# x ahead of ca on one DMA queue, a qkv bias loaded as a row, batch 0's ga spread by TensorE, and a tail in halves of tokens

## The chip, the cores and the metric

The kernel runs on one core of one Trainium2 chip. The metric is the device time of one execution in microseconds, the median over runs. Engines: TensorE (PE, with its weight loads PEld), VectorE (DVE), ScalarE (ACT), GpSimd (POOL), and SyncE (SP), which issues almost all DMAs.

## The reference

Four batches of 512 tokens with 512 features, float32: an AdaLN block of single-head attention and a feed-forward with a routed low-rank part.

```
mod = silu(c) @ wmod                      # c (4, 512), wmod (512, 6*512) -> sa, ca, ga, sb, cb, gb per batch
ga = sign(ga) * max(|ga|, 0.25)           # sign(0) = 1; gb alike
h = layernorm(x) * (1 + ca) + sa
q, k, v = split(h @ Wqkv + bqkv)          # 128 features each
x = x + ga * (softmax(q k^T / sqrt(128)) v @ Wo + bo)
h = layernorm(x) * (1 + cb) + sb
e = argmax(h @ gate_w.T + expert_bias)    # 4 experts, the first of equals
x = x + gb * (h @ W_up.T + lora_B[e] (lora_A[e] h))   # rank 8
```

## The kernel before, in words

Tokens lie on partitions in four tiles of 128 (index t); features in four blocks of 128 (index kt). Products keep float32 precision by splitting each factor into a high part (float32r, made by ScalarE as a copy from PSUM, `h1_high`, `pt_high`, `o_high`, `h2_high`) and a low part (the rest, made by VectorE, `h1_low`, `pt_low`, `o_low`, `h2_low`, `wup_low`), and three matmuls for each pair (`products`, L346).

Each engine has one program, written out by hand, and works through it in order; semaphores tie them. The eight PSUM banks are handed from use to use by the list in `psum_plan`: `open_bank` waits until the bank's earlier content has been read. A step of batch b is: LN1 (statistics on DVE, power on GpSimd, scale on ACT or DVE), `x1_transposes`, h1, `qkv`, `scores`, `maxima` (DVE) and `softmax` (ACT), `p_transposes`, `pv`, `out_projection`, `residual` and `ln2_moments` (DVE) on an xs to which GpSimd has added ga*bo (`add_output_bias`), LN2 (`ln2_deviation` on GpSimd, `ln2_normalise` on ACT), `x2_transposes`, h2, `gate_and_lora_a`, `z_to_tokens`, `choose_expert` (a chain of small DVE instructions), `z_transposes`, `up` (h2 @ W_up), `lora_up`, `gate_ffn` (times gb, DVE) and `outputs` (GpSimd's add, then a store by SP). In the loop over b = 1 to 3 batch b's attention is interleaved on TensorE with batch b-1's feed-forward.

At the head, the six sections of wmod are loaded, 1 MB each: ca from ScalarE's DMA queue, all else from SP's, in the order c, four tiles of x[0], Wqkv, sa, Wqkv, bqkv, x[1], ga, then, each behind a wait for a finished use of its buffer, sb, Wo, bo, W_up, x[2], the gate and LoRA weights, cb, gb. `modulation(g)` multiplies a section by silu(c); `modulation_columns` transposes the result, `add_parts` sums the parts into columns (`mod_sum`). bqkv comes as a column `bqkv_col` and is added to the transposed sa shift in `qkv_shift`.

The gates: `gate_columns` (four small DVE instructions, L1002 to L1010) applies the floor, `gate_to_rows` transposes, `gate_rows_evacuate` copies the rows from PSUM, SP writes them to DRAM and reads them back spread over all partitions (`write_gate`, `spread_gate`). GpSimd multiplies Wo and bo by the spread ga (`output_weights` L1325, `output_bias` L1330), ACT takes its high part (`wo_high`), GpSimd the low part. For gb, `gate_columns` stands before batch 1's maxima and before `ffn_shift_rows` and `gate_shift` (`gz_sum`).

VectorE also copies lora_B three times side by side (L1223) and splits sb (L992, L994) after h1_low(1). In the last batch the x2 transposes and h2 go tile by tile, and the router works on all four tiles at once; GpSimd adds tiles 0 to 2 and VectorE tile 3 (L1291).

## Time and profile before

| | |
|---|---|
| median of 3 runs | 198.2 us (198.16 to 198.65) |
| profiled execution, all | 198.7 us |
| its span, first to last instruction | 197.0 us |
| TensorE busy | 176.2 us (89%), 923 matmuls |
| VectorE | 136.3 us (69%), 328 instructions |
| ScalarE | 90.4 us (46%) |
| GpSimd | 80.7 us (41%) |
| mean granted TensorE clock | 0.974 |
| DMA | 19.47 MB, mean 99 GB/s |

Times are microseconds from the start of the span. A matmul's busy time overlaps that of the next one, so the distance of their starts is what each costs; "<-" after an idle time names what ended it. The clock is a share of 2.4 GHz; its lower level is 1.2 GHz. The difference between the profiled execution's 198.7 and its span of 197.0 lies outside the span.

### The profile page before, as it was taken

How to read it: one execution, taken by the hardware profiler on the slowest of the kernel's cores; microseconds unless marked ns; L12 is line 12 of the kernel's file. 1: busy time of each engine (PE TensorE's matmuls, PEld its weight loads, DVE VectorE, ACT ScalarE, POOL GpSimd, SP SyncE). 2: the span in 40 equal slices, each digit the busy share in tenths (PEclk: the TensorE clock that was granted, in tenths of full speed). 3: DMA queues.
4: the chain of work that ended last, by engine and by line, in shares of the span. 5: the costliest groups of instructions: out<-in, count | busy, mean ns of one | idle time of the engine just before them, and what ended most of it. 6: DMA issues, size and time to landing. Idle time of an engine off the chain costs nothing.

```text
span 197.0 us, 2766 instructions
## 1 busy us (share of the span) xinstructions
PE 176.2 (89%) x923; PEld 136.8 (69%) x923; DVE 136.3 (69%) x328; ACT 90.4 (46%) x170; POOL 80.7 (41%) x107
## 2 busy tenths in 40 slices
PE   6486999969997987997999999999999999997990
PEld 6362675758756765885888788878878888675760
DVE  0544953899598999897885478569576466975443
ACT  2146305876037677804546596103665601572110
POOL 3262320003982794054388940016694000614242
PEclk9958999999999999999999999999999999999996
DMA  5989992941005000400021500000230000101204
GB/s 183 405 301 398 309 359 51 325 144 68 0 21 194 3 2 0 156 6 3 2 102 57 161 3 0 0 0 18 92 133 27 2 0 0 45 13 53 106 21 192
DMA packets 12789, 19.47 MB, mean 99 GB/s; under 512 B 3256, under 2 KB 3768, under 8 KB 12776
## 3 DMA queue, kind: packets, MB, share of 16 engines
q1 hardware_dynamic: 12248, 18.26, 26.2%
q10 hardware_dynamic: 528, 1.05, 1.6%
q8 instruction: 7, 0.11, 0.2%
q14 instruction: 6, 0.05, 0.1%
HBM read 15.09 MB, written 4.21 MB: 98 GB/s over the span
## 4 chain that ended last, share of the span: by engine, by line
PE 47%; ACT 2%; DVE 2%; issue 1%; DVEq 0%
PE bank L346 33%; PE bank L558 2%; PE bank L464 2%; PE bank L491 2%; PE bank L518 1%; ACT h2hi L811 1%; PE bank L521 1%; PE bank L499 1%; PE bank L449 1%; PE bank L446 1%; PE bank L443 1%; PE bank L420 1%; DVE xs L1291 1%; PE bank L538 1%; ACT xn_p L792 1%
## 5 line engine op out<-in xcount | busy, mean ns | idle before, releaser
L346 PE MATMUL bank<-wup_lo,h2hi 128*128 128x512 f32 x64 | 26.6, 416 | 0.0
L1348 POOL TENSOR_TENSOR rstd<-var_eps,neg_half 128x1 f32<-128x1 f32 x16 | 8.8, 550 | 42.9 <-DVE var_eps L1118 42.9
L792 ACT ACTIVATE xn_p<-xs,shift,rstd 128x512 f32<-128x512 f32 x16 | 13.1, 818 | 26.6 <-POOL shift L1351 26.6
L346 PE MATMUL bank<-wup_hi,h2hi 128*128 128x512 f32 x64 | 25.3, 395 | 0.0
L346 PE MATMUL bank<-wup_hi,h2lo 128*128 128x512 f32 x64 | 25.2, 394 | 0.0
L1363 POOL TENSOR_TENSOR xs<-xs,f_gb 128x512 f32<-128x512 f32 x15 | 19.2, 1292 | 10.8 <-DVE f_gb L1168 10.8
L346 PE MATMUL bank<-h1lo,wqkv_hi 128*128 128x512 f32 x48 | 19.7, 411 | 1.2 <-ACT wqkv_hi L785 1.2
L1340 POOL TENSOR_TENSOR xs<-xs,gabo 128x512 f32<-128x512 f32 x16 | 20.2, 1304 | 0.1
L346 PE MATMUL bank<-h1hi,wqkv_hi 128*128 128x512 f32 x48 | 19.0, 395 | 0.0
L346 PE MATMUL bank<-h1hi,wqkv_lo 128*128 128x512 f32 x48 | 18.9, 394 | 0.0
L1325 POOL TENSOR_TENSOR wo_ga<-wo_raw,ga_bc 128x512 f32<-128x512 f32 x4 | 5.2, 1294 | 28.3 <-DMA ga_bc<-gates_dram 28.3
L1107 DVE SCALAR_TENSOR_TENSOR xs<-bank,row_inv,xs 128x512 f32<-128x512 f32 x16 | 12.0, 747 | 6.2 <-PE bank L346 2.6
L1081 DVE TENSOR_REDUCE row_max<-bank 128x1 f32<-128x512 f32 x16 | 10.9, 683 | 5.1 <-PE bank L449 5.1
L918 DVE BATCH_NORM_STATS2 stats<-xs 128x6 f32<-128x512 f32 x16 | 10.1, 679 | 5.8 <-DMA xs<-in_L_attn_x_dram 5.8
L346 PEld LDWEIGHTS bank<-wup_hi,h2hi 128*128 128x128 f32 x64 | 12.0, 188 | 2.8
L346 PEld LDWEIGHTS bank<-wup_lo,h2hi 128*128 128x128 f32 x64 | 12.1, 189 | 2.3
L346 PEld LDWEIGHTS bank<-wup_hi,h2lo 128*128 128x128 f32 x64 | 12.1, 189 | 2.1
L1168 DVE TENSOR_TENSOR f_gb<-bank,gb_bc 128x512 f32<-128x512 f32 x16 | 10.6, 686 | 3.2 <-PE bank L558 3.2
L755 ACT ACTIVATE xn_p<-bank,neg_max 128x512 f32<-128x512 f32 x16 | 11.0, 688 | 3.1 <-DVE neg_max L1083 3.0
L1046 DVE SCALAR_TENSOR_TENSOR h1lo<-bank,modT_ca,h1hi 128x512 fp32r<-128x512 f32 x16 | 11.2, 744 | 1.6 <-ACT h1hi L711 1.5
L1090 DVE TENSOR_TENSOR plo<-bank,phi 128x512 fp32r<-128x512 f32 x16 | 10.0, 681 | 3.1 <-ACT phi L763 3.0
L1114 DVE BATCH_NORM_STATS2 stats<-xs 128x6 f32<-128x512 f32 x16 | 11.1, 695 | 1.1 <-DVE xs L1107 0.5
(173 smaller groups left out, 411.8 us busy)
## 6 DMA issues: line engine op xcount, KB each, us to landing
out_dram<-xs SPq DMA_DIRECT2D x16, 256.0 KB, 2.0
xs<-in_L_wmod_dram SPq DMA_DIRECT2D x3, 1024.0 KB, 8.0
xs<-in_L_attn_x_dram SPq DMA_DIRECT2D x3, 1024.0 KB, 8.3
stage<-in_L_wmod_dram SPq DMA_DIRECT2D x2, 1024.0 KB, 5.9
stage<-in_L_wmod_dram ACTq DMA_DIRECT2D x1, 1024.0 KB, 5.9
xs<-in_L_attn_x_dram SPq DMA_DIRECT2D x4, 256.0 KB, 5.8
f_gb<-in_L_ffn_W_up_dram SPq DMA_DIRECT2D x1, 1024.0 KB, 10.8
ga_bc<-gates_dram SPq DMA_DIRECT2D x4, 256.0 KB, 3.6
```

Of the source, the lines that this page charges most:

```text
L346: mm = nc.tensor.matmul(dst, w, m, start=first and i == 0, stop=last and i == total - 1)
L755: nc.scalar.activation(xn2_p[:, t, :], at("S", b, t)[:], ACT.Exp, bias=neg_max[:, t:t + 1], scale=SCORE_SCALE, accum_out=row_sum[:, t:t + ...
L792: nc.scalar.activation(xn2_p[:, t, :], xs[:, b, t, :], ACT.Identity, bias=shift[:, 1, t:t + 1], scale=rstd[:, 1, t:t + 1]).then_inc(S["xn2 ...
L918: nc.vector.bn_stats(stats[:, 0, t, :], xs[:, b, t, :]).then_inc(S["ln1_stats"], 1)
L1046: nc.vector.scalar_tensor_tensor(h1lo[:, kt, :], at("x1T", b, kt)[:], modT["ca"][:, kt, b:b + 1], h1hi[:, kt, :].bitcast(F32), ALU.mult, A ...
L1081: nc.vector.reduce_max(row_max[:, t:t + 1], at("S", b, t)[:], AX_X).then_inc(S["max_ready"], 1)
L1090: nc.vector.tensor_tensor(plo[:, :, q], at("PT", b, t)[:].rearrange("p (k q) -> p k q", k=NT), phi[:, :, q].bitcast(F32), ALU.subtract).th ...
L1107: nc.vector.scalar_tensor_tensor(xs[:, b, t, :], at("Y", b, t)[:], row_inv[:, t:t + 1], xs[:, b, t, :], ALU.mult, ALU.add).then_inc(S["x2_ ...
L1114: nc.vector.bn_stats(stats[:, 1, t, :], xs[:, b, t, :]).then_inc(S["ln2_stats"], 1)
L1168: nc.vector.tensor_tensor(f_gb[:, n % 4, :], at("F", b, t)[:], gb_bc[:, b % 2, :], ALU.mult).then_inc(S["f_gb_ready"], 1)
L1340: nc.gpsimd.tensor_tensor(xs[:, b, t, :], xs[:, b, t, :], gabo[:], ALU.add).then_inc(S["xb_ready"], 1)
L1363: nc.gpsimd.tensor_tensor(xs[:, b, t, :], xs[:, b, t, :], f_gb[:, n % 4, :], ALU.add).then_inc(S["out_ready"], 1)
```

## The change

- SP loads x[0] in two halves, then ca, all on one queue; batch 0's fourth tile is transposed after `modulation(0)`, with two warming matmuls after each of the other tiles.
- bqkv is loaded as a row into four of eight partitions of `bqkv_rows`, the other four zero, and added by VectorE to the sa shift before its transposes (the add on the columns and ScalarE's copy are gone).
- x[2] is loaded ahead of Wo, bo and W_up; two of batch 2's LN1 statistics move ahead of batch 0's maxima.
- Batch 0's spread ga is made by four matmuls (a gate column broadcast as weights, the identity moving) and a ScalarE copy; its DMA round is gone, and `wo_high(0)` moves up. sb's sums come before v_low(0); ga's rows are copied after all of pt_low(0).
- gb's gate math, transposes and row copy move into iteration 1 of the loop, behind h1_low, `up(0, 1)` and pt_low.
- In the last batch `gate_and_lora_a`, `z_to_tokens`, `choose_expert`, `z_transposes` and their copies work on halves of tokens; ScalarE normalises tiles 0 and 1 before the first h2_high and tile 3 before the third; the order of `up` is cut finer; VectorE adds tiles 2 and 3 itself.

```diff
-        (1, "S", 0, 0), (3, "S", 0, 1), (0, "S", 0, 2), (2, "S", 0, 3), (4, "V", 0), (6, "modT", 2), (5, "gate_row", "ga"),
+        (1, "S", 0, 0), (3, "S", 0, 1), (0, "S", 0, 2), (2, "S", 0, 3), (4, "V", 0), (6, "modT", 2), (6, "ga_bc"), (5, "gate_row", "ga"),
...
-            order += [(f[1], "gate_row", "gb")]
+            order += [(f[2], "gate_row", "gb")]
...
             sp.dma_start(c_row[:], c).then_inc(c_in, 16)
-            for t in range(NT):
-                sp.dma_start(xs[:, 0, t, :], x_v[0, :, t, :]).then_inc(x0_in[t], 16)
+            for i in range(2):
+                sp.dma_start(xs[:, 0, 2 * i:2 * i + 2], x_v[0, :, 2 * i:2 * i + 2, :]).then_inc(x0_in[i], 16)
+            load_section("ca")
             load_wqkv((0, 1))
             load_section("sa")
             load_wqkv((2, 3))
-            sp.dma_start(bqkv_col[:], bqkv.rearrange("(j d) -> d j", d=D),
-                         allow_slow_non_contiguous=True).then_inc(bqkv_in, 16)
+            sp.wait_ge(S["bqkv_zero"], 1)
+            sp.dma_start(bqkv_rows[0:B, :], bqkv.partition_broadcast(B)).then_inc(bqkv_in, 16)
             sp.dma_start(xs[:, 1], x_v[1]).then_inc(x_in[1], 16)
             load_section("ga")
             wait_used(0)
             load_section("sb")
+            wait_used(1)
+            sp.dma_start(xs[:, 2], x_v[2]).then_inc(x_in[2], 16)
             sp.dma_start(wo_raw[:], wo).then_inc(wo_in, 16)
             sp.dma_start(bo_bc[:], bo.partition_broadcast(P)).then_inc(bo_in, 16)
             sp.dma_start(raw["wup"][:], wup.rearrange("(o p) h -> p o h", p=P)).then_inc(wup_in, 16)
-            wait_used(1)
-            sp.dma_start(xs[:, 2], x_v[2]).then_inc(x_in[2], 16)
             sp.dma_start(ga_rows[0:E, :], gate_w).then_inc(ga_rows_in, 16)
             sp.dma_start(ga_rows[E:GZ, :], lora_a.rearrange("e r h -> (e r) h")).then_inc(ga_rows_in, 16)
...
             write_gate(0)
-            spread_gate(0, 0)
             spread_gate(0, 1)
...
+            def first_gate_everywhere():
+
+                dst = open_bank("ga_bc")
+                pe.wait_ge(S["gate_col_ready"], 1)
+                for kt in range(NK):
+                    mm = nc.tensor.matmul(dst[:, kt * P:(kt + 1) * P], gate_col[:, 0, kt, 0:1].to_broadcast([P, P]), ident[:],
+                                          start=True, stop=True)
+                mm.then_inc(S["ga_bc_psum"], 1)
...
+            def last_gate_and_lora_a(half):
+
+                dst = open_bank("gz", LAST, half)
+                h2_tile(2 * half + 1)
+                q = slice(2 * half * P, (2 * half + 2) * P)
+                for kt in range(NK):
+                    w = gzw[:, kt, :, :].rearrange("p a g -> p (a g)")
+                    nc.tensor.matmul(dst[0:2 * GZ, q], w, h2hi[:, kt, q], start=kt == 0, stop=False)
+                    mm = nc.tensor.matmul(dst[0:2 * GZ, q], w, h2lo[:, kt, q], start=False, stop=kt == NK - 1)
+                mm.then_inc(S["gz_psum"], 1)
...
-            first_x1_transposes(range(NT))
+            for t in range(NT - 1):
+                first_x1_transposes((t,))
+                keep_warm(bank[4], 2)
             modulation(0)
+            first_x1_transposes((NT - 1,))
             first_modulation_columns(0)
...
             p_transposes(0, (0, 1))
+            first_gate_everywhere()
             gate_to_rows("ga")
             p_transposes(0, (2, 3))
...
-                if b == 1:
-                    gate_to_rows("gb")
...
                 up(b - 1, 1)
+                if b == 1:
+                    gate_to_rows("gb")
                 pv(b)
...
             last_x2_transposes(2)
-            up(b, 0)
+            up(b, 0, (0, 1))
             last_x2_transposes(3)
+            up(b, 0, (2, 3))
+            last_gate_and_lora_a(0)
             up(b, 1, (0, 1))
-            gate_and_lora_a(b)
+            z_to_tokens(b, 0)
+            last_gate_and_lora_a(1)
             up(b, 1, (2, 3))
-            z_to_tokens(b)
-            up(b, 2)
-            z_transposes(b)
-            up(b, 3, (0,))
+            z_to_tokens(b, 1)
+            up(b, 2, (0, 1))
+            z_transposes(b, 0)
+            up(b, 2, (2, 3))
             lora_up(b, 0)
             lora_up(b, 1)
-            up(b, 3, (1,))
+            up(b, 3, (0, 1))
+            z_transposes(b, 1)
+            up(b, 3, (2,))
             lora_up(b, 2)
-            up(b, 3, (2, 3))
+            up(b, 3, (3,))
             lora_up(b, 3)
...
-            nc.scalar.dma_start(raw["ca"], wmod_v[SECTION["ca"]]).then_inc(mod_in["ca"], 16)
...
-            act.wait_ge(S["qb_row_psum"], 1)
-            nc.scalar.activation(qb_row[:], at("qb_row")[0:2 * B, 0:3 * D], ACT.Copy).then_inc(S["qb_row_ready"], 1)
             qkv_evacuate(0)
             modulation_rows(2)
             softmax(0, (0, 1, 2))
             v_evacuate(0)
             softmax(0, (3,))
-            pt_high(0)
-            h1_high(1)
+            pt_high(0, (0, 1))
+            act.wait_ge(S["ga_bc_psum"], 1)
+            nc.scalar.activation(ga_bc[:, 0, :], at("ga_bc")[:], ACT.Copy).then_inc(S["ga_bc_ready"], 1)
+            pt_high(0, (2, 3))
+            h1_high(1, (0, 1))
+            wo_high(0)
+            h1_high(1, (2, 3))
             o_high(0)
-            wup_high((0, 1))
-            wo_high(0)
-            wup_high((2, 3))
+            wup_high(range(NK))
             ln2_normalise(0, (0, 1))
...
+                    gz_evacuate(b)
                 else:
-                    for t in range(NT):
-                        ln2_normalise(b, (t,))
-                        last_h2_high(t)
-                gz_evacuate(b)
-            zT_evacuate(LAST)
+                    ln2_normalise(b, (0, 1))
+                    last_h2_high(0)
+                    ln2_normalise(b, (2,))
+                    last_h2_high(1)
+                    ln2_normalise(b, (3,))
+                    last_h2_high(2)
+                    last_h2_high(3)
+            for half in range(2):
+                gz_evacuate(LAST, half)
+            for half in range(2):
+                zT_evacuate(LAST, half)
...
+            def qkv_shift_row():
+                dve.wait_ge(S["qb_row_psum"], 1)
+                dve.wait_ge(bqkv_in, 16)
+                nc.vector.tensor_tensor(qb_row[:], at("qb_row")[0:2 * B, 0:3 * D], bqkv_rows[:],
+                                        ALU.add).then_inc(S["qb_row_ready"], 1)
+
             def qkv_shift():
                 dve.wait_ge(S["qb_col_psum"], 1)
-                nc.vector.tensor_reduce(qb_sum[:], at("qb_col")[:, 0:3 * 2 * B].rearrange("p (j a b) -> p j b a", j=3, a=2),
-                                        AX_X, ALU.add).then_inc(S["qb_sum_ready"], 1)
-                dve.wait_ge(S["qb_sum_ready"], 1)
-                dve.wait_ge(bqkv_in, 16)
-                nc.vector.tensor_tensor(qb[:], qb_sum[:], bqkv_col[:].unsqueeze(2).to_broadcast([P, 3, B]),
-                                        ALU.add).then_inc(S["qb_ready"], 1)
+                nc.vector.tensor_reduce(qb[:], at("qb_col")[:, 0:3 * 2 * B].rearrange("p (j a b) -> p j b a", j=3, a=2),
+                                        AX_X, ALU.add).then_inc(S["qb_ready"], 1)
...
             second_ln1_normalise()
+            qkv_shift_row()
             qkv_shift()
             qk_low(0)
+            ln1_stats(2, (0, 1))
             maxima(0)
             add_parts("ga")
             gate_columns("ga")
+            add_parts("sb")
             v_low(0)
-            pt_low(0, (0,))
+            pt_low(0)
             gate_rows_evacuate("ga")
-            pt_low(0, (1, 2, 3))
-            add_parts("sb")
             h1_low(1)
             split_sb()
...
-            ln1_stats(2, (0, 1, 2, 3))
+            ln1_stats(2, (2, 3))
             ln1_moments(2)
             h2_low(0)
             qk_low(1)
-            gate_columns("gb")
             ffn_shift_rows()
...
             for b in range(1, B):
                 last = b == LAST
                 maxima(b)
-                if b == 1:
-                    gate_rows_evacuate("gb")
                 v_low(b)
                 if not last:
                     h1_low(b + 1)
+                if b == 1:
+                    gate_columns("gb")
                 pt_low(b)
+                if b == 1:
+                    gate_rows_evacuate("gb")
                 choose_expert(b - 1)
...
+                    for t in range(3):
+                        residual(b, t)
+                        ln2_moments(b, t)
+                        if t == 1:
+                            gate_ffn(b - 1, 0)
                     last_h2_low(0)
...
+                    residual(b, 3)
+                    ln2_moments(b, 3)
                     last_h2_low(1)
                     last_h2_low(2)
-                    gate_ffn(b - 1, 1)
                     last_h2_low(3)
...
-            choose_expert(LAST)
-            for t in range(NT):
+                    for t in range(1, NT):
+                        gate_ffn(b - 1, t)
+            choose_expert(LAST, 0)
+            choose_expert(LAST, 1)
+            gate_ffn(LAST, 0)
+            gate_ffn(LAST, 1)
+            for t in (2, 3):
                 gate_ffn(LAST, t)
+                n = NT * LAST + t
+                dve.wait_ge(S["f_gb_ready"], n + 1)
+                nc.vector.tensor_tensor(xs[:, LAST, t, :], xs[:, LAST, t, :], f_gb[:, n % 4, :],
+                                        ALU.add).then_inc(last_out_ready, 1)
...
-                pool.wait_ge(ga_bc_in[b % 2], 16 * (b // 2 + 1))
                 if b == 0:
+                    pool.wait_ge(S["ga_bc_ready"], 1)
                     pool.wait_ge(wo_in, 16)
                     pool.wait_ge(bo_in, 16)
                 else:
+                    pool.wait_ge(ga_bc_in[b % 2], 16 * ((b + 1) // 2))
...
-                ln2_deviation(b, (0, 1))
-                outputs(b - 1, (0,))
-                ln2_deviation(b, (2,))
                 if not last:
+                    ln2_deviation(b, (0, 1))
+                    outputs(b - 1, (0,))
+                    ln2_deviation(b, (2,))
                     outputs(b - 1, (1,))
-                ln2_deviation(b, (3,))
-                if last:
-                    outputs(b - 1, (1,))
-                if not last:
+                    ln2_deviation(b, (3,))
                     split_output_weights(b + 1)
-                outputs(b - 1, (2, 3))
-            outputs(LAST, (0, 1, 2))
+                    outputs(b - 1, (2, 3))
+                else:
+                    ln2_deviation(b, range(NT))
+                    outputs(b - 1, range(NT))
+            outputs(LAST, (0, 1))
```

`z_to_tokens`, `choose_expert`, `z_transposes`, `gz_evacuate` and `zT_evacuate` take an optional half and then work on tiles 2*half and 2*half + 1; VectorE's first instruction is now a memset of `bqkv_rows`.

## Rows read from the trace of the kernel before

**Rows 1.** Windows of 2 us: each engine's busy time, clock granted, DMA share, GB/s.
```profile
8.00:10.00 2.00, 0.10 (x1) 0.10 (x2) 1.86 (x7) 0.81 (x1) 1.15 (x3) 0.83 1.06 404
...
12.00:14.00 2.00, 2.00 (x10) 1.71 (x9) 0.55 (x1) 0.85 (x2) 1.23 (x2) 0.50 0.66 171
...
18.00:20.00 2.00, 0.81 (x6) 0.60 (x6) 1.96 (x3) 2.00 (x5) 1.01 (x2) 1.00 1.03 386
```

**Rows 2.** TensorE's waits: total us, times, longest us.
```profile
PE bank L411 <- ACT xn L845: 3.4, 2, 2.9
PE bank L420 <- DVE mod_sum L956: 1.6, 1, 1.6
...
PE bank L491 <- ACT xn_p L792: 1.4, 1, 1.4
PE bank L383 <- DVE gz_sum L1030: 1.4, 1, 1.4
PE bank L346 <- DVE o_lo L1099: 1.2, 1, 1.2
...
PE bank L518 <- DVE h2lo L1061: 1.1, 1, 1.1
PE bank L499 <- ACT xn_p L792: 0.9, 2, 0.5
```

**Rows 3.** DMA queues from 3 to 4 us: packets, MB, share (q10 is ScalarE's).
```profile
q10 hardware_dynamic: 183, 0.37, 99.9%
```

**Rows 4.** Timeline of the start: start us, us, engine, line, what.
```profile
6.90 0.69 DVE L918 BATCH_NORM_STATS2 stats<-xs 128x6 f32<-128x512 f32 x1 [5.79 <-DMA xs<-in_L_attn_x_dram]
...
11.62 0.81 ACT L845 ACTIVATE xn<-xs,shift,rstd 128x512 f32<-128x512 f32 x1 [0.19 <-POOL shift L1308]
...
14.38 1.92 PE L360 MATMUL bank<-stage,silu_wide 128*32 128x512 f32 x8
...
21.88 1.06 PE L360 MATMUL bank<-xs,silu_wide 128*32 128x512 f32 x8
```

**Rows 5.** Timeline of VectorE and GpSimd, 45 to 75 us.
```profile
45.63 1.24 DVE L994 TENSOR_TENSOR sb_wide<-mod_sum,sb_wide 128x32 fp32r<-128x32 f32 x1
...
46.88 0.47 DVE L1223 COPY xn<-lora_b_raw 128x128 f32<-128x128 f32 x3
...
68.98 0.85 DVE L1002 SCALAR_TENSOR_TENSOR gate_tmp<-mod_sum 128x16 f32<-128x16 f32 x1
69.76 1.33 DVE L1004 TENSOR_SCALAR gate_tmp<-mod_sum 128x16 f32<-128x16 f32 x1
...
74.73 0.68 DVE L1081 TENSOR_REDUCE row_max<-bank 128x1 f32<-128x512 f32 x1
...
68.50 1.31 POOL L1330 TENSOR_TENSOR gabo<-bo_bc,ga_bc 128x512 f32<-128x512 f32 x1
```

**Rows 6.** Line L1142, all batches: duration ns min/median/max, first and last start.
```profile
L1142 DVE TENSOR_TENSOR bank<-z_sum,z_arg x4: 299/300/682, 86.6 to 185.8; 128x128 f32<-128x128 f32 x4
```

**Rows 7.** Timeline of GpSimd and VectorE before batch 0's LN2.
```profile
45.54 1.29 POOL L1325 TENSOR_TENSOR wo_ga<-wo_raw,ga_bc 128x512 f32<-128x512 f32 x1 [19.76 <-DMA ga_bc<-gates_dram]
...
52.83 0.75 DVE L1107 SCALAR_TENSOR_TENSOR xs<-bank,row_inv,xs 128x512 f32<-128x512 f32 x1 [2.33 <-POOL xs L1340]
```

**Rows 8.** Timeline of iteration 1, VectorE and TensorE (pv(1)'s first matmul).
```profile
85.02 0.45 DVE L1128 TENSOR_REDUCE z_sum<-bank 128x144 f32<-128x288 f32 x1
...
90.86 0.68 DVE L1099 TENSOR_TENSOR o_lo<-bank,o_hi 128x512 fp32r<-128x512 f32 x1
...
85.88 0.39 PE L346 MATMUL bank<-plo,v_hi 128*128 128x512 f32 x1
```

**Rows 9.** Timeline of the end: GpSimd, VectorE and SP's stores.
```profile
190.88 2.49 POOL L1363 TENSOR_TENSOR xs<-xs,f_gb 128x512 f32<-128x512 f32 x2
...
192.35 1.57 DVE L1291 TENSOR_TENSOR xs<-xs,f_gb 128x512 f32<-128x512 f32 x1
...
190.94 3.81 SPq L323 DMA_DIRECT2D out_dram<-xs  x4
```

163 lines of the change are left out of this document (77 added, 86 removed).

## The prediction

> **What bounds the kernel now.** I read the windows of two microseconds first [rows 1], for TensorE's share and its granted clock, then TensorE's waits, then the timeline of each engine around each wait. From 92 us to 169 us TensorE has no gap at all (the chain of waits is one run of its matmuls there), so an edit counts only where TensorE stands still, runs at the low clock, or ends. [Rows 2] are the places: 3.4 us for the first normalised tiles, 1.6 for `mod_sum` (x1 transposes of batch 1 behind sb's sums), 1.4 for batch 0's LN2, 1.4 for `gz_sum` (the gb transposes and bank 7 behind DVE's gate math), 1.2 for batch 1's `o_lo`, and 2.0 for the last h2 tiles. In [rows 1] the reader sees the clock: 0.83 in 8 to 10 us, 0.50 in 12 to 14 us (1.2 of 2.4 GHz), 1.00 again in 18 to 20 us with TensorE only 0.81 of 2.00 us busy.
>
> **The start: -4.3 us.** ScalarE's queue carries ca and takes 99.9% of the DMA engines from 3 to 4 us [rows 3]; x waits behind it, and VectorE's first statistics start at 6.90 us [rows 4]. With x ahead on one queue, half of batch 0 (0.52 MB) flows from some 2.6 us at the 404 GB/s of [rows 1], 1.3 us. Now ca's 1.05 MB and the first tile's 0.26 need 3.2 of the 6.90 us, so 3.7 us are issue and latency, and the half lands at 3.7 + 1.3 = 5.0; I take 4.8, as ca's issue and ramp are also gone (estimate). Statistics, GpSimd's pow and ScalarE's scale keep their pace, so the third tile, ready at 11.62 + 0.81 = 12.4 us [rows 4], is ready at 10.3. ca, 1.05 MB behind x's 1.05, lands near 8.6 us (now 6.7): later, yet in time. modulation(0) no longer waits for the fourth tile's transposes: it starts at 11.0 instead of 14.38. Its eight matmuls took 1.92 us at the low clock; the same eight took 1.06 at 21.88 us at full clock [rows 4]. TensorE's gaps are now at most 0.9 us with two warming matmuls between tiles, against the idle 7.0 to 9.3 us after which the clock fell, and [rows 1] show 40% busy time at full clock. So it ends at 12.1 instead of 16.3: -4.2, and 0.1 more from the column transposes at full clock. The fourth tile's transposes fit into ScalarE's copy of the modulation rows. Bounds: -4.6 (x lands at 4.4) to -2.2 (low clock all through: 1.9 for the eight, 0.6 on transposes, then 0.6 on the first columns, less what gaps absorb).
> Does the gain reach 37 us? Everything there follows TensorE's own queue. sb, the last load it needs, has 7.1 MB through the queue: 17.6 us at 404 GB/s, landed at 21; modulation(2) would run near 27. bqkv as a row takes 384 four-byte pieces out of the queue; they are the reason for 171 GB/s in 12 to 14 us [rows 1], about 1.1 us of DMA time. Nobody waits for what is behind them: 0. The bias add moves from after the transposes (0.17 us) to before, onto a DVE that idles there: 0. x2 ahead of Wo, bo and W_up costs nothing: W_up is used at 46 us.
>
> **Batch 0's ga: -0.2.** sb's sums come before v_low, so bank 6 is free early and the 1.6 us wait goes. But `gate_rows_evacuate("ga")` now stands behind all four pt_low, and the transposes of x1 of kt=3 need its bank 5: they start at 42.9 us, pv at 43.35 instead of 43.53. The four spreading matmuls (0.45 us) and ScalarE's copy (0.6 us, delays pt_high of tile 2) lie inside that.
>
> **The same edit, at LN2: x2_transposes(0) comes 1.3 later, at 63.4 instead of 62.05** (VectorE sets it, so the -0.2 is lost in it). GpSimd starts wo_ga at 45.54 [rows 7], held by the DMA trip; now near 40.5. Its chain (wo_lo behind ScalarE's wo_hi at 43.3, gabo, four adds of 1.25 us) then fills 43.3 to 50.9 without a gap. Taken alone the residual, 52.83 [rows 7], could start at 51.0 and TensorE's wait of 1.4 us is gone: -1.45. What speaks against it: VectorE's split of sb and its three copies of lora_B now fall into 45.4 to 50.9. [Rows 5] show what happens there: L994 (0.17 us of work) took 1.24 us and ended with GpSimd's wo_ga; L1002 and L1004, back to back, took 0.85 and 1.33 us, each ending with one GpSimd instruction. The three copies took 0.47 us in all, at a time when GpSimd was idle. No row shows a copy beside GpSimd: between 0.16 us and 1.25 us each. They pass 128 elements in 0.16 us, where the two-input L1142 needs 0.30 [rows 6], so they run in a quick form like L1004, and L1004 waited: I take 1.25. Five instructions (cast, subtract, three copies) from 45.4 on end with GpSimd's boundaries, the last at 50.9, when it falls silent; that also caps the loss. Then o_low ends at 51.6 (was 47.95), out_projection(0) starts at 51.7 instead of 50.24; Y tiles 1 to 3 wait for wup_low in banks 4, 6, 5; wup_low ends at 54.15, and the first residual starts there, 1.3 later than now. The four tiles keep their pace: +1.3.
> The Trainium skill, page "SBUF — State Buffer", section "Who interferes with whom", says that copy, cast and tensor_scalar in a two-port mode, and instructions with two SBUF inputs, exclude GpSimd's for their whole length, and that the later one waits. For L994, L1002 and L1004 this trace agrees (1.24, 0.85, 1.33 us); for the copies no run here shows it yet. By that rule the sum stands as I make it; by one-port copies it would be 190.4.
>
> **gb's gate math leaves the head of batch 1: from +1.3 to -0.95.** It took DVE 4.6 us from 68.98, one GpSimd instruction per step [rows 5]. ffn_shift_rows then waits for ScalarE's fb_hi, which stands behind wo_high(1) and LN1 of batch 2 and comes at 72.7 even with LN2 1.3 us late, because half of batch 2's statistics (1.25 us) went into a DVE gap before batch 0's maxima. So maxima(1), now at 74.73 [rows 5], start at 73.75; softmax and x1's transposes follow, and TensorE is 0.95 ahead at 79 us. Without the waiting copies it would be 2.9 ahead.
>
> **Inside iteration 1: +1.45, so +0.5.** gate_columns after h1_low: 0.6 us, GpSimd idle. The rows' copy waits for transposes that TensorE does only after up(0,1), at 85.88 [rows 8]; it ends near 87.05, and choose_expert starts then instead of at 85.02: +2.0. L1142 is inside: 0.68 us now, 0.30 when GpSimd is silent [rows 6]: -0.4, and 0.15 from wakes. z_transposes(0) waits 0.6 us on TensorE. o_low, at 90.86 [rows 8], is DVE's next bound and already TensorE's wait of 1.2 us: every bit is paid. Bounds 0 (slack that I don't see) to +2.0. gates reach DRAM 8.5 us later; SP's gb_bc and ga_bc(2) behind them too, GpSimd's wo_ga(2), gabo and ln1 offsets for batch 3 then end at 97.6 and ScalarE reaches LN2's last tile at its old distance: 0, with 0.1 us to spare.
>
> **The tail: -2.05.** ScalarE's order brings the last h2_high 0.8 us forward (the second normalise no longer stands behind h2_high(0); DVE's residual 3 is 0.6 later). TensorE still waits some 1.5 us for the fourth tile, and ends 0.9 earlier. 16 gz matmuls of 256 columns: 0.12 us each if they go by columns (0: as now), 0.23 if not (+1.8, the upper bound). The half chains of choose_expert (2.2 us each, twice 8 more small instructions) are hidden behind up(3,2) and up(3,3), even with 1.2 us of waits for GpSimd's outputs. DVE's last add took 1.57 us [rows 9], 1.0 of it for GpSimd's add of tile 2, until 193.37; with tiles 2 and 3 both on DVE it is 0.65, and the last store isn't second in SP's line, 0.38. 0.9 + 0.65 + 0.5 = 2.05. Bounds -2.5 to -0.3.
>
> **Sum.** -4.3 + 0.5 - 2.05 = -5.85. The profiled execution had a span of 197.0 and 198.7 us in all, its median runs 198.2: spans of 191.2, median 198.2 - 5.85 = 192.4.
>
> **Rivals.**
> - The copies don't wait (a DVE copy gets between GpSimd's adds). For: 0.16 us each today. Against: L1004. x2_transposes at 60.6, 2.0 less in all: 190.4. Chance 0.18.
> - The clock falls in the start's gaps. For: it fell after 2.3 us idle, and TensorE is half idle from 7 to 10 us. 1.0 on modulation(0) and transposes, up to 1.1 on qkv's first matmuls: 193.5 to 194.5. Chance 0.15.
> - Tail or iteration 1 at their upper bounds: 256 columns cost 0.23 us each, or the DMA trip behind the gates reaches x2_transposes(1): 194. Chance 0.14.
> - Slower: the low clock stays for qkv of batch 0. Each us of dense work costs one more; the start's 1.0 and 4.85 us of such work eat all, which needs a clock of 0.5 until about 26 us; to 28 us it is 199.5. Before, it came back at 16.1 us, after 4.6 us of nearly full work. Chance 0.03.
> - The start's gain stops at a load (ga, sb or x1 late in the single queue). It would need sb 6 us later than worked out; then 196 to 198.2. Chance 0.05.
> - The forecast, 191.4 to 193.3: 0.45.
>
> Range 190.0 to 194.9. Telling from no change takes about 0.3%, 0.6 us. Faster 0.94, same 0.03, slower 0.03.
>
> **What would show it.** modulation(0)'s eight matmuls at 11.0 for 1.06 us, clock 1.00 throughout; the first qkv matmul near 15.3 (now 19.6). Take the start's shift of 4.3 off for the rest: L1223's copies about 3.7 us in all and TensorE waiting 1.6 us for o_lo before out_projection(0) (if they are 0.5 us, the first rival); no wait for gz_sum; the copy of gb's rows waiting on TensorE's transposes, then TensorE waiting for zst and 1.5 us or more for o_lo in batch 1; one wait of some 1.5 us before the last tile's transposes; DVE's last two adds at 0.55 to 0.7 us. The prediction is wrong if sb's or x's landing times differ, or if TensorE shows a clock of 0.50 after 8 us.

## The result, and the profile after

The changed kernel takes 195.31 us (median of four runs, 195.11 to 195.52), the kernel before 198.43 on the same chip: ratio 0.9841 [0.9815, 0.9866]. It is faster, as forecast, by 1.6% with an interval clear of 1, but by 3.1 us and not by 5.85, and 192.4 with its range of 190.0 to 194.9 was wrong: the time lies 0.4 us above the range. None of the rivals had named this time either. The profiled execution took 195.13 us, span 193.3; against the span of 197.0 before, 3.7 us are gone. The sum had put the span at 191.15, so 2.15 of the 2.9 us that I missed are in its terms. The other 0.75 are what lies around them: the profiled execution of before was 0.5 us over its median, the changed one 0.2 under it, and 0.1 is outside the spans (rounded).

TensorE's waits after the change, the answer to [rows 2] (total us, times, longest us):

```profile
PE bank L432 <- ACT xn_p L785: 2.5, 2, 2.0
PE bank L349 <- DVE o_lo L1140: 2.0, 2, 1.6
PE bank L335 <- POOL low_rows L1418: 1.6, 1, 1.6
PE bank L511 <- ACT xn_p L822: 1.4, 1, 1.4
...
PE bank L432 <- DVE gates L1055: 0.9, 1, 0.9
...
PE bank L423 <- ACT xn L876: 0.5, 1, 0.5
```

The wait of 1.4 us for `gz_sum` is gone, as meant, and of the 3.4 us for the first normalised tiles 0.5 is left. The 1.6 us that x1's transposes of batch 1 waited for `mod_sum` became 0.9, now for the copy of ga's rows (`gates`). But a wait of 2.0 us stands at the top that was not there: x1's transposes of batch 2 behind batch 1's softmax. That is where most of the missing time is, and the reader can follow it down.

**The start** went as worked out. TensorE's and VectorE's timelines of the changed kernel, which answer to [rows 4]:

```profile
4.69 0.69 DVE L957 BATCH_NORM_STATS2 stats<-xs 128x6 f32<-128x512 f32 x1 [3.19 <-DMA xs<-in_L_attn_x_dram]
...
11.31 1.06 PE L363 MATMUL bank<-stage,silu_wide 128*32 128x512 f32 x8
...
15.68 0.47 PE L349 MATMUL bank<-h1lo,wqkv_hi 128*128 128x512 f32 x1 [1.20 <-ACT wqkv_hi L815]
```

and its windows of 2 us, which answer to [rows 1]:

```profile
8.00:10.00 2.00, 1.52 (x15) 1.33 (x13) 1.27 (x5) 1.40 (x2) 1.63 (x5) 1.00 1.06 395
...
12.00:14.00 2.00, 2.00 (x18) 1.47 (x15) 0.57 (x4) 1.21 (x4) 0.47 (x2) 1.00 1.06 381
```

Ahead of qkv the granted clock is 1.00 (2.4 GHz) where it was 0.83 and 0.50, the eight modulation matmuls take 1.06 us in place of 1.92, and qkv's first matmul comes at 15.68 in place of 19.62 us: 3.94 us, where I had 4.3.

**LN2 of batch 0.** VectorE and GpSimd from 36 to 50 us, which answer to [rows 5] and [rows 7]:

```profile
42.00 0.36 DVE L1031 CAST sb_wide<-mod_sum 128x32 fp32r<-128x32 f32 x1
42.39 0.19 DVE L1033 TENSOR_TENSOR sb_wide<-mod_sum,sb_wide 128x32 fp32r<-128x32 f32 x1
...
42.59 3.72 DVE L1270 COPY xn<-lora_b_raw 128x128 f32<-128x128 f32 x3
46.23 0.68 DVE L1140 TENSOR_TENSOR o_lo<-bank,o_hi 128x512 fp32r<-128x512 f32 x1
...
49.22 0.74 DVE L1148 SCALAR_TENSOR_TENSOR xs<-bank,row_inv,xs 128x512 f32<-128x512 f32 x1
...
36.74 1.27 POOL L1374 TENSOR_TENSOR wo_ga<-wo_raw,ga_bc 128x512 f32<-128x512 f32 x1 [14.88 <-ACT ga_bc L894]
...
42.40 5.06 POOL L1389 TENSOR_TENSOR xs<-xs,gabo 128x512 f32<-128x512 f32 x4
```

GpSimd's `wo_ga` starts 8.8 us earlier. The three copies, 0.47 us before, now take 3.72, one of GpSimd's adds each, and with them `o_low(0)` is late. x2_transposes(0) start at 58.43 us, 3.62 earlier than before: of the start's 3.94, 0.32 is lost here. TensorE's line in the kernel before, and in the changed one:

```profile
62.05 1.97 PE L491 MATMUL bank<-ident,xn_p 128*128 128x128 f32 x16 [1.45 <-ACT xn_p L792]
...
58.43 1.97 PE L503 MATMUL bank<-ident,xn_p 128*128 128x128 f32 x16 [0.49 <-ACT xn_p L822]
```

**The head of batch 1.** The same two engines from 66 us:

```profile
67.86 0.76 DVE L1081 SCALAR_TENSOR_TENSOR lbw<-stage,low_rows,bank 32x512 fp32r<-32x512 f32 x1 [3.64 <-ACT stage L915]
...
68.85 2.39 DVE L1075 TENSOR_SCALAR gz_bias<-gz_sum,eb_col 72x4 f32<-72x4 f32 x1
71.15 0.68 DVE L1122 TENSOR_REDUCE row_max<-bank 128x1 f32<-128x512 f32 x1
...
66.16 5.05 POOL L1389 TENSOR_TENSOR xs<-xs,gabo 128x512 f32<-128x512 f32 x4
```

The gate math is gone from here and VectorE is idle 3.64 us ahead of `ffn_shift_rows`. Then `gz_bias`, the addition of the expert bias on 72x4 elements, takes 2.39 us. It starts 0.2 us after GpSimd's third add has begun and ends with the fourth (the adds' 5.05 us in four equal parts). In the kernel before it took 0.23 us:

```profile
72.37 1.20 DVE L1010 SCALAR_TENSOR_TENSOR gate_col<-gate_tmp 128x16 f32<-128x16 f32 x1
...
74.59 0.23 DVE L1034 TENSOR_SCALAR gz_bias<-gz_sum,eb_col 72x4 f32<-72x4 f32 x1
...
71.00 4.99 POOL L1340 TENSOR_TENSOR xs<-xs,gabo 128x512 f32<-128x512 f32 x4
```

Behind `gz_bias` in VectorE's queue stand the maxima, behind these softmax, behind this TensorE (2.0 us). ScalarE waits for it as well: its copy of gz, which needs `gz_bias` and stands ahead of softmax in its queue, was idle 3.50 us for it. The maxima start at 71.15, 3.58 us earlier than in [rows 5], which is what had been ahead anyway (3.62): moving the gate math out of here gave nothing.

**Iteration 1**, which answers to [rows 8]; the copy of the gb rows now waits for TensorE:

```profile
82.94 0.68 DVE L1055 COPY gates<-bank 4x512 f32<-4x512 f32 x1 [1.06 <-PE bank L386]
83.55 0.43 DVE L1172 TENSOR_REDUCE z_sum<-bank 128x144 f32<-128x288 f32 x1
...
88.98 0.69 DVE L1140 TENSOR_TENSOR o_lo<-bank,o_hi 128x512 fp32r<-128x512 f32 x1
```

From x1_transposes(2) (72.97 us, 76.55 before) to out_projection(1) 1.71 us are lost, and out_projection(1) is 1.87 us ahead of before. In the kernel before, and in the changed one:

```profile
91.80 0.47 PE L346 MATMUL bank<-wo_lo,o_hi 128*128 128x512 f32 x1 [1.20 <-DVE o_lo L1099]
...
89.93 0.47 PE L349 MATMUL bank<-wo_lo,o_hi 128*128 128x512 f32 x1 [1.60 <-DVE o_lo L1140]
```

**The tail**, which answers to [rows 9]: VectorE's last add starts at 190.15 and ends at 190.84, where the last one of before ended near 193.9. TensorE has one wait of 1.37 us before the last tile's transposes. The eight gz matmuls of 256 columns of each half start 0.12 us apart, where those of 512 columns were 0.23 apart before: here the cost went by columns. The tail gave 1.98 us.

```profile
190.15 0.69 DVE L1339 TENSOR_TENSOR xs<-xs,f_gb 128x512 f32<-128x512 f32 x1
```

### The profile page after: what moved, and what is told of

Its sections match the earlier page's. It is cut to its first block, busy times and chain, and to the rows that moved or that the text cites. A ratio compares the mean times of both kernels' runs of the same rounds, so it can differ in the third digit from the quotient of the medians.

```text
span 193.3 us, 2846 instructions
## 1 busy us (share of the span) xinstructions
PE 177.2 (92%) x951; PEld 139.1 (72%) x951; DVE 139.6 (72%) x339; ACT 91.3 (47%) x172; POOL 79.6 (41%) x106
## 4 chain that ended last, share of the span: by engine, by line
PE 45%; DVE 4%; issue 1%; ACT 1%; POOL 1%; DVEq 0%; POOLq 0%
PE bank L349 31%; PE bank L476 2%; PE bank L503 2%; PE bank L579 1%; DVE xs L1148 1%; DVE stats L1155 1%; PE bank L527 1%; PE bank L529 1%; PE bank L461 1%; PE bank L455 1%; PE bank L458 1%; PE bank L432 1%; PE bank L557 1%; DVE f_gb L1213 1%; ACT h2hi L841 1%
## 5 line engine op out<-in xcount | busy, mean ns | idle before, releaser
L1412 POOL TENSOR_TENSOR xs<-xs,f_gb 128x512 f32<-128x512 f32 x14 | 17.9, 1293 | 7.2 <-DVE f_gb L1213 7.2
L957 DVE BATCH_NORM_STATS2 stats<-xs 128x6 f32<-128x512 f32 x16 | 10.2, 679 | 3.2 <-DMA xs<-in_L_attn_x_dram 3.2
L349 PEld LDWEIGHTS bank<-h1lo,wqkv_hi 128*128 128x128 f32 x48 | 9.0, 188 | 4.0 <-ACT wqkv_hi L815 1.4
## 6 DMA issues: line engine op xcount, KB each, us to landing
xn_p<-in_L_attn_Wqkv_dram SPq DMA_DIRECT2D x4, 192.0 KB, 8.8
```

The costliest lines, as they stand in the source:

```text
L349: mm = nc.tensor.matmul(dst, w, m, start=first and i == 0, stop=last and i == total - 1)
L957: nc.vector.bn_stats(stats[:, 0, t, :], xs[:, b, t, :]).then_inc(S["ln1_stats"], 1)
L1412: nc.gpsimd.tensor_tensor(xs[:, b, t, :], xs[:, b, t, :], f_gb[:, n % 4, :], ALU.add).then_inc(S["out_ready"], 1)
```

## The experiments

Each kernel below is the changed kernel with the edit shown, unless it says otherwise; "..." marks lines of an edit left out. They ran on four chips, each group with its own runs of the kernel before, 198.4 to 198.8 us in the median, so a difference of a few tenths between two kernels may lie in the chips.

**1. gz_sum left in PSUM.** If `gz_bias` is slow because both its operands are in SBUF beside GpSimd's adds, an operand in PSUM frees it.

```diff
-nc.vector.tensor_reduce(gz_sum[:], at("gzb")[0:2 * GZ, 0:2 * B]...)
-nc.vector.tensor_scalar(gz_bias[:], gz_sum[:], eb_col[:], None, ALU.add)
+nc.vector.tensor_reduce(at("gzb")[0:2 * GZ, 64:64 + B], at("gzb")[0:2 * GZ, 0:2 * B]...)
+nc.vector.tensor_scalar(gz_bias[:], at("gzb")[0:2 * GZ, 64:64 + B], eb_col[:], None, ALU.add)
```

The plan of PSUM banks also keeps the bank until `gz_bias` has been computed.

Expected: 

> The changed kernel, with gz_sum kept in PSUM (bank 7, columns 64 to 67), so that gz_bias's tensor_scalar reads no SBUF tensor. Theory (GpSimd keeps VectorE's SBUF-to-SBUF tensor_scalar out): gz_bias takes 0.2 us instead of 2.39, batch 1's maxima start near 69.0 instead of 71.15, and TensorE's 1.98 us wait for the first softmax tile falls under 0.3. The end is 1.9 to 2.2 us earlier: 193.2 of 195.3. Rival (the time was lost somewhere else in that stretch, for example in batch 1's scores or fb_hi): maxima start at 69.0, but the end moves by less than 0.5 us.

Measured 192.74 us (192.71 to 193.07), ratio 0.9699 [0.9638, 0.976]: 2.57 less than the changed kernel, 0.5 less than expected. VectorE's timeline:

```profile
68.78 0.22 DVE L1075 TENSOR_SCALAR gz_bias<-bank,eb_col 72x4 f32<-72x4 f32 x1
68.92 0.68 DVE L1122 TENSOR_REDUCE row_max<-bank 128x1 f32<-128x512 f32 x1
```

The maxima come 2.23 us earlier, the wait of 2.0 us for softmax is gone, and the time falls by that and a little more. The cause of the largest part of the miss is shown: one small instruction. On a second chip the same kernel gave 192.83 (192.62 to 192.99).

> The changed kernel with gz_sum left in PSUM, for a second chip: 192.5 to 193.1, 2.5 us below the changed kernel.

**2. The three copies on ScalarE**, after `wup_high`, in place of VectorE.

```diff
-nc.vector.tensor_copy(lora_b_rep[:, :, a, :], lora_b_raw[:])
+nc.scalar.activation(lora_b_rep[:, :, a, :], lora_b_raw[:], ACT.Copy)
```

Expected: 

> The changed kernel, with lora_B's three copies made by ScalarE behind wup_high, where it stands idle. Theory (the copies wait for one GpSimd add each, 3.3 us in all): o_low(0) starts as soon as o_high is done, near 43.5 instead of 46.23, batch 0's residual near 47.6 instead of 49.22, x2_transposes(0) 1.1 us earlier (TensorE's waits of 0.4, 0.2 and 0.5 us are gone). The end moves by less than that as long as gz_bias waits for GpSimd's four adds in batch 1, whose end depends on ScalarE and GpSimd: 194.3 to 195.2. Rival (copies are slow by themselves there): they are slow on ScalarE too, and nothing moves.

Measured 194.77 (194.26 to 194.86), 0.54 less. `o_low(0)` starts at 44.06 in place of 46.23 and the first residual at 48.02 in place of 49.22, so the copies did hold LN2. x2_transposes(0) start 1.15 us earlier. But half of it is given back at once, because GpSimd's adds in batch 1 come only 0.52 us earlier (65.64 against 66.16) and `gz_bias` again ends with the fourth: it takes 2.41 us here too, and TensorE's wait for softmax grows to 2.65 us. After it the granted clock fell, as the windows show:

```profile
70.00:72.00 2.00, 0.00 (x0) 0.00 (x0) 1.97 (x4) 1.15 (x2) 0.69 (x1) 1.00 0.00 0
72.00:74.00 2.00, 1.55 (x8) 1.57 (x9) 1.75 (x6) 1.98 (x7) 0.00 (x0) 0.50 0.00 0
```

**3. The gb rows copied by ScalarE**, between its pt_high(1) and o_high(1), so that nothing on VectorE waits for them.

```diff
-                if b == 1:
-                    gate_rows_evacuate("gb")
...
                 pt_high(b)
+                if b == 1:
+                    act.wait_ge(S["gate_row_psum"], 2)
+                    nc.scalar.activation(gates[:, 1, :], at("gate_row", "gb")[0:B, :], ACT.Copy)
                 o_high(b)
```

Expected: 

> The changed kernel, with gb's rows copied from PSUM by ScalarE between pt_high(1) and o_high(1). Theory (the wait of 1.06 us for TensorE's transposes and the 0.68 us copy stand in the chain choose_expert, batch 3's statistics, o_low): choose_expert starts at 81.9 instead of 83.55, z_transposes has no wait, o_low(1) starts near 87.3, TensorE's wait for it falls from 1.60 to 0. The end 1.6 to 1.7 us earlier: 193.6. Rival (TensorE's wait for o_low has another cause, ScalarE's o_high or batch 3's data): o_low doesn't move, 195.3.

Measured 194.81 (193.89 to 195.93), 0.5 less and not 1.7, and with this spread not clear of no change. The first half of the theory held: z_sum starts at 81.63 in place of 83.55, and the wait for o_lo(1) is 0.7 in place of 1.6. The second half did not: 1.3 us come back at LN2 of batch 1. TensorE's waits and GpSimd's timeline:

```profile
PE bank L503 <- ACT xn_p L822: 1.8, 2, 1.3
...
90.12 1.29 POOL L1375 TENSOR_TENSOR wo_ga<-wo_raw,ga_bc 128x512 f32<-128x512 f32 x1 [19.06 <-DMA ga_bc<-gates_dram]
91.37 1.29 POOL L1380 TENSOR_TENSOR gabo<-bo_bc,ga_bc 128x512 f32<-128x512 f32 x1
92.63 1.02 POOL L1347 TENSOR_TENSOR rstd<-var_eps,neg_half 128x4 f32<-128x4 f32 x1
```

GpSimd's `wo_ga` for batch 2 waits for ga_bc(2), a DMA that stands in SyncE's queue behind gb's trip through DRAM; gabo, LN1's offsets of batch 3 and then LN2's of batch 1 (from 94.67 us) stand behind it on GpSimd. In the changed kernel GpSimd is at LN2's offsets at nearly the same time (94.47), but TensorE comes 1.9 us later to out_projection(1), which hid this.

**4. The three edits together.** Expected: 

> All three edits together. Theory: the waits are in series on TensorE's path, so they add up: 195.3 - 2.1 - 1.1 - 1.7 = 190.4; with something taken by the next bound 190.4 to 191.5. Rival (one bound behind all three): no better than the best of them alone, 193.2.

Measured 191.36 (191.03 to 192.51), ratio 0.9645 [0.9567, 0.9724]: 3.95 less than the changed kernel, more than the 3.6 that the three gave singly.

**5. The start alone, on the kernel before.** Expected: 

> The kernel before with only the new start: x in halves and ca ahead on SyncE, and the order of the first transposes that goes with it. My account: the first modulation matmul comes 3 us earlier and runs at the granted clock of 1.00 from its beginning, and all of it stays to the end, as nothing later in the kernel before waits for a load or for the wall clock: 3.9 us less than before, 194.3 to 194.8. Rival: a wait further on (the gates of batch 0, LN2) is filled by what was hidden in the late start, and 2 us or less are left (196.4 or more).

```diff
-            for t in range(NT):
-                sp.dma_start(xs[:, 0, t, :], x_v[0, :, t, :])
+            for i in range(2):
+                sp.dma_start(xs[:, 0, 2 * i:2 * i + 2], x_v[0, :, 2 * i:2 * i + 2, :])
+            load_section("ca")
...
-            first_x1_transposes(range(NT))
+            for t in range(NT - 1):
+                first_x1_transposes((t,))
+                keep_warm(bank[4], 2)
             modulation(0)
+            first_x1_transposes((NT - 1,))
...
-            nc.scalar.dma_start(raw["ca"], wmod_v[SECTION["ca"]]).then_inc(mod_in["ca"], 16)
```

Measured 195.19 (194.75 to 195.27), ratio 0.9834 [0.9798, 0.9871], span 193.1. That is 0.4 us above the range I gave and far from the rival's 196.4. The span is 3.9 us below the 197.0 of before, as large as the start's gain; by the medians of this chip it is 3.6. The changed kernel's 195.31 and its span of 193.3 differ from this by no more than the runs do. So everything else in the change adds up to about nothing: what the tail gives (1.98) is lost in iteration 1 (1.71) and at LN2 of batch 0 (0.32), and the head of batch 1 gives nothing.

**6. The tail of before, in the changed kernel** (whole tiles; the functions of the tail as they were).

```diff
-                    if b == LAST and t >= 2:
-                        sp.wait_ge(last_out_ready, t - 1)
+                    if b == LAST and t == NT - 1:
+                        sp.wait_ge(last_out_ready, 1)
...
-            up(b, 0, (0, 1))
+            up(b, 0)
...
```

Expected: 

> The changed kernel with the tail of the kernel before (whole tiles, not halves of tokens). My account: the tail gave 1.98 us of span, so the time is 2.0 us above the changed kernel, 197.1 to 197.5. Rival: the tail's gain was partly a gain of the work ahead of it (the last expert), and the difference is under 1 us.

Ten runs, 197.04 to 198.32, median 198.15, above my 197.1 to 197.5. They form two groups: two runs at a mean clock of 0.998 took 197.04 and 197.25 us, eight at 0.984 to 0.986 took 197.89 to 198.32. The profiled run, one of the eight, shows a clock of 0.50 from 74 to 76 us, after the softmax wait of 1.98 us and the transposes behind it. The changed kernel's two runs at a mean clock of 0.997 took 195.11 and 195.13, so at that clock the tail is worth 1.9 to 2.1 us, as forecast. The other 1.0 us goes with the lower mean clock; that it fell at the same place in the seven runs without a profile is inferred.

**7. The gate math early in iteration 1**, on kernel 4: gb's gate columns between the maxima and v_low (and no longer after h1_low), the turn to rows right after x1_transposes(2).

```diff
                 maxima(b)
+                if b == 1:
+                    gate_columns("gb")
                 v_low(b)
```

Expected: 

> The changed kernel with gz_sum in PSUM, the three copies and the gb rows on ScalarE, and besides gb's gate columns between maxima(1) and v_low(1), with the turn to rows after x1_transposes(2). My account: the DMA trip of gb's gates starts some 4 us earlier, so that GpSimd and with it LN2 of batch 1 are no longer late (the wait of 1.3 us there goes) and what is left of the wait for o_lo goes too: 0.4 to 1.1 us below the kernel with the three edits, 190.3 to 191.0. Rival: that wait is VectorE's own work, not the trip's, and the time is the same, 191.2 to 191.6.

Measured 190.29 (190.19 to 190.67), ratio 0.9598 [0.9578, 0.9619], the best kernel of all: 5.0 us below the changed one. GpSimd's wo_ga(2) is done before LN1's offsets, which come at 84.09 in place of 88.70 us in kernel 4 (92.63 in kernel 3), and TensorE's wait at LN2 of batch 1, 0.47 us in kernel 4, is gone:

```profile
84.09 1.02 POOL L1347 TENSOR_TENSOR rstd<-var_eps,neg_half 128x4 f32<-128x4 f32 x1 [0.72 <-DVE var_eps L971]
```

Between the maxima and v_low each of the four steps takes 0.17 us: none of them waits.

**8. Batch 0's ga by DMA again.** Expected: 

> The changed kernel with batch 0's ga spread by DMA again, as before. My account: the spreading by TensorE costs 0.99 us of TensorE and spares the wait for the DMA trip, but what then ends the wait in front of LN2 is VectorE's three copies behind GpSimd's adds, so that taking it back moves the time by no more than 0.4 us either way: 194.9 to 195.7. Rival: the early ga is what brings residual(0, 0) forward, and without it the time is 1.5 us longer (196.8).

```diff
             write_gate(0)
+            spread_gate(0, 0)
             spread_gate(0, 1)
...
-            first_gate_everywhere()
```

ScalarE's `wo_high(0)` also goes back to its old place between the halves of `wup_high`.

Measured 195.0 (193.66 to 196.24), span 193.4 in the profile. In it `gz_bias` takes 2.39 us as in the changed kernel, the three copies take 0.47 us again (they start at 41.59, and GpSimd's wo_ga only at 43.42), and the first residual starts at 49.48, 0.26 later. So the trade is nearly even there. But its runs scatter over 2.6 us, and the spans of 191.8 and 192.0 in two of them are left without a profile.

**9. The gate math back in its old place**, ahead of `ffn_shift_rows`.

```diff
+            gate_columns("gb")
             ffn_shift_rows()
...
-                if b == 1:
-                    gate_columns("gb")
```

Expected: 

> The changed kernel with gb's gate math back in front of ffn_shift_rows. My account: VectorE is idle from 64.15 to 67.86 us there, and gz_bias waits for GpSimd's adds to 71.2 us anyway, so the gate math costs nothing there, and the late place in iteration 1 is freed of part of its waits: 194.8 to 195.4. Rival (the one in my prediction's sum): each of its instructions waits for a GpSimd add, maxima(1) comes 2.3 us later and the time is 197.6.

Measured 193.72 (193.55 to 193.84), ratio 0.9764 [0.973, 0.9798]: 1.6 less than the changed kernel, more than either account gave. VectorE and GpSimd:

```profile
63.99 0.85 DVE L1041 SCALAR_TENSOR_TENSOR gate_tmp<-mod_sum 128x16 f32<-128x16 f32 x1
64.77 1.33 DVE L1043 TENSOR_SCALAR gate_tmp<-mod_sum 128x16 f32<-128x16 f32 x1
...
67.39 1.22 DVE L1049 SCALAR_TENSOR_TENSOR gate_col<-gate_tmp 128x16 f32<-128x16 f32 x1
68.65 0.76 DVE L1081 SCALAR_TENSOR_TENSOR lbw<-stage,low_rows,bank 32x512 fp32r<-32x512 f32 x1
...
69.63 0.23 DVE L1075 TENSOR_SCALAR gz_bias<-gz_sum,eb_col 72x4 f32<-72x4 f32 x1
69.77 0.68 DVE L1122 TENSOR_REDUCE row_max<-bank 128x1 f32<-128x512 f32 x1
...
66.02 5.04 POOL L1388 TENSOR_TENSOR xs<-xs,gabo 128x512 f32<-128x512 f32 x4
```

The four steps take 4.6 us of VectorE and the kernel is still faster, because VectorE has nothing to do until 67.86 us and because `gz_bias`, 0.8 us later, now falls right before the end of GpSimd's third add (near 69.8 us, by 66.02 and four adds in 5.04) and ends with it. The maxima start 1.38 us earlier.

This place is not a matter of luck. The last gate step ends with one of GpSimd's adds (68.61 us, where the second ends near 68.54), and `ffn_shift_rows` and `gz_sum` behind it take the 1.0 us that bring `gz_bias` to 0.2 us before the next end. The kernel before shows the same at 73.57 and 74.59 us (third add until about 74.74), and so does kernel 5, with adds from 66.84 us in 4.99:

```profile
70.41 0.23 DVE L1037 TENSOR_SCALAR gz_bias<-gz_sum,eb_col 72x4 f32<-72x4 f32 x1
```

So in these three kernels the gate math, by waiting itself, put `gz_bias` near the end of an add.

**10. A probe on kernel 1**: extra small SBUF to SBUF instructions beside GpSimd's adds. Expected: 

> A probe on the kernel with gz_sum in PSUM: small SBUF to SBUF instructions of VectorE beside GpSimd's adds of 1.24 us: tensor_scalar with its scalar from a column in SBUF (as gz_bias), tensor_scalar with an immediate, and a copy. It does extra work that no output uses. If the wait of 2.4 us belongs to the form with a column for scalar, that form takes up to 2.5 us and the others up to 1.3 us; if it belongs to the moment at which the instruction comes, all of them show waits between 0.1 and 1.3 us, with 2.4 us in none or in any of the forms.

```diff
+nc.vector.tensor_scalar(probe[0:2 * GZ, 1, :], probe[0:2 * GZ, 0, :], 1.0, None, ALU.add)
+nc.vector.tensor_scalar(probe[0:2 * GZ, 2, :], probe[0:2 * GZ, 0, :], eb_col[:], None, ALU.add)
+nc.vector.tensor_copy(probe[0:2 * GZ, 3, :], probe[0:2 * GZ, 0, :])
```

```profile
64.93 1.15 DVE L1090 TENSOR_SCALAR probe<-probe,eb_col 72x4 f32<-72x4 f32 x1 [0.87 <-POOL gabo L1400]
65.99 1.34 DVE L1088 TENSOR_SCALAR probe<-probe 72x4 f32<-72x4 f32 x1
...
106.59 1.07 DVE L1090 TENSOR_SCALAR probe<-probe,eb_col 72x4 f32<-72x4 f32 x1
...
143.51 1.07 DVE L1088 TENSOR_SCALAR probe<-probe 72x4 f32<-72x4 f32 x1
144.50 1.33 DVE L1092 COPY probe<-probe 72x4 f32<-72x4 f32 x1
```

All three forms wait, each until the next end of a GpSimd instruction; none waits for two. The time of its one run is 192.85 us, within kernel 1's 192.71 to 193.07: these waits cost nothing that shows.

**11 and 12. Form or moment of gz_bias.** Kernel 11 adds an immediate 0 in place of the column, so it leaves the expert bias out. Kernel 12 puts two more sums ahead of gz_sum.

```diff
-nc.vector.tensor_scalar(gz_bias[:], gz_sum[:], eb_col[:], None, ALU.add)
+nc.vector.tensor_scalar(gz_bias[:], gz_sum[:], 0.0, None, ALU.add)
```

Expected of 11: 

> The changed kernel with gz_bias = gz_sum + 0 by an immediate in place of the column eb_col in SBUF; it leaves the expert bias out. If the long wait belongs to the form with a column for scalar, gz_bias takes 1.1 to 1.3 us and the time falls by 1.2 us (194.1). If it belongs to the moment, gz_bias again takes 2.4 us and the time is that of the changed kernel, 195.1 to 195.5.

Expected of 12: 

> The changed kernel with two more sums of the same 72x8 from PSUM (no output uses them) ahead of gz_sum, 0.16 us each: gz_bias is ready some 0.4 us later, nearer to the end of GpSimd's add at 69.9 us. If the moment decides, as in the kernel with the early gate math (ready 0.17 us before an end of an add: 0.23 us), it ends with this add, maxima(1) comes near 70.0 in place of 71.15, and the time is 1.1 us shorter (194.2). If the form decides, it ends at 71.2 as before and the time is that of the changed kernel.

```profile
68.64 2.41 DVE L1075 TENSOR_SCALAR gz_bias<-gz_sum 72x4 f32<-72x4 f32 x1
```

Kernel 11 measured 195.51 (193.75 to 196.09), and `gz_bias` took 2.41 us: a column in place of an immediate is excluded as the cause. Kernel 12 measured 196.0 (194.8 to 196.43) and does not decide: its two sums took 0.23 us together, gz_bias was ready at 68.82 and not near 69.8, and took 2.25 us.

```profile
68.48 0.23 DVE L1073 TENSOR_REDUCE gz_fill<-bank 72x4 f32<-72x8 f32 x2
...
68.82 2.25 DVE L1079 TENSOR_SCALAR gz_bias<-gz_sum,eb_col 72x4 f32<-72x4 f32 x1
```

**13. Kernel 7 with batch 0's ga by DMA.** Expected: 

> The best kernel so far (gz_sum in PSUM, copies and gb rows on ScalarE, gate math before v_low) with batch 0's ga by DMA again. Here no copies of VectorE wait, so the DMA trip itself should end the wait in front of LN2: residual(0, 0) 1.2 to 1.5 us later, against 1.4 us of TensorE spared (the eight matmuls and the wait for mod_sum). My account: 190.0 to 190.9, no difference over 0.4 us. Rival: the trip is on the path with its whole length, 191.7; or the spared TensorE time stays, 189.0.

Measured 191.66 (191.4 to 192.0), 1.4 us more than kernel 7: my account (190.0 to 190.9) missed, and the rival, the trip on the path with its whole length (191.7), was right. The first residual starts at 49.30 in place of 47.32 and waits 2.29 us for GpSimd's first add:

```profile
49.30 0.75 DVE L1153 SCALAR_TENSOR_TENSOR xs<-bank,row_inv,xs 128x512 f32<-128x512 f32 x1 [2.29 <-POOL xs L1388]
```

So the spreading by TensorE, with the early `wo_high(0)` that goes with it, is worth 1.4 us once VectorE's copies are out of GpSimd's way, and nothing that kernel 8 could show while they are in it.

## Why the prediction missed

By the terms of its sum, in us of span:

| term | predicted | measured |
|---|---|---|
| the start | -4.3 | -3.94 |
| the same edit, at LN2 of batch 0 | +1.3 | +0.32 |
| gb's gate math leaves the head of batch 1 | -2.25 | +0.04 |
| inside iteration 1 | +1.45 | +1.71 |
| iteration 1 to the last out_projection | 0 | +0.15 |
| the tail | -2.05 | -1.98 |
| sum | -5.85 | -3.7 |

**The step that failed: "gb's gate math leaves the head of batch 1: from +1.3 to -0.95."** I had maxima(1) follow `ffn_shift_rows` at once and booked `gz_bias` at the quarter microsecond it had before. In the same text I said that small SBUF to SBUF instructions of VectorE wait for GpSimd, and counted this for the copies, but not for the one such instruction that stayed behind when the gate math left. It took 2.39 us and ate 2.2 us; kernel 1 takes it back to 0.22 us and gives 2.57 of time. The list of what waits was wrong, and so would have been my size for it: by my count of one GpSimd instruction each, `gz_bias` would have cost at most 1.25 us, and it waited for two. In the old order the gate math, in step with GpSimd's adds, had brought it just ahead of an end (experiment 9); I moved that away with the gate math.

Without the softmax wait, 195.31 - 2.57 = 192.74 lies 0.3 us from the forecast. That is closer than the working deserves: the other terms were 0.98 us too pessimistic at LN2 and 0.84 too optimistic in all the rest, and by luck these cancel. Neither of the two signs of being wrong that I named, a landing time or a clock of 0.50 after 8 us, came; I had set no sign for the term that failed.

**The LN2 term was right in mechanism and 1.0 us too large.** The copies waited as forecast (3.72 us against "about 3.7"), which excludes the first rival. But the copies ended with GpSimd's third add (46.31 us), not with the fourth (47.46), on which I had capped the loss: the cast ended with gabo at 42.36 us after 0.36, and the subtraction slipped in behind it in 0.19, as the xs adds began.

**The start**: the mechanism held in each part (first statistics at 4.69 against 4.8, clock 1.00 throughout, 1.06 us for the eight). It was 0.36 too large; modulation(0) came at 11.31 against 11.0. The rivals of a falling clock and of a late load did not happen, and kernel 5 shows the gain nearly whole to the end. How much of it is the order of the loads and how much the warming matmuls, no kernel separates; the rows put 2.2 us at x's arrival (first statistics at 4.69 in place of 6.90) and 0.86 at the eight matmuls.

**Batch 0's ga, "The four spreading matmuls (0.45 us)"**, was mis-sized: they show as eight records, 0.99 us from their start at 34.87 to the next group, after a wait of 0.44 us for `mod_sum`. pv(0) came at 39.91, not 39.0. As forecast, VectorE sets LN2, so this lay beside the path.

**Iteration 1 and the tail** came within 0.3 and 0.1 us; kernel 6 shows the tail by itself. The bias as a row and the place of x[2] among the loads, which I had at 0, were not run by themselves; with the rest of the change they add up to about nothing (kernel 5).

I gave -5.85 from the span of one execution that stood 0.5 us over its own median, and subtracted it from the median; that alone is up to half a microsecond of optimism, if what that execution took more is in the waits and the clock dip that I counted as gains of the change. No run shows that it is.

**What stays open** is why `gz_bias` waited for two of GpSimd's adds in seven of the profiled kernels (2.25 to 2.41 us; the changed one, 2, 3, 6, 8, 11 and 12), while copies, gate steps and the probe waited for one. A column or an immediate doesn't decide (kernel 11). The moment matters: 0.2 us before the end of an add it took 0.23 us (before, kernels 5 and 9), 0.1 to 0.3 us after the start of one it took two adds (the seven). But the moment can't be all: the first copy of lora_B, 0.19 us after the start of GpSimd's first add, took 1.22 us, and the probe, three times about 0.2 us after the start of a GpSimd instruction, 1.07 to 1.15, one each. Kernel 12 failed to shift the moment. That the runs of kernels 8 and 11 with spans of 191.8 to 192.0 us are ones in which `gz_bias` got through is an inference from their size and not seen.
